# Last cross attention: the output product from rounded halves, and one softmax normalisation handed from VectorE to ScalarE

## The reference

```python
q = (x @ Wq).reshape(B, Sq, h, d).transpose(0, 2, 1, 3)
k = (context @ Wk).reshape(B, -1, h, d).transpose(0, 2, 1, 3)
v = (context @ Wv).reshape(B, -1, h, d).transpose(0, 2, 1, 3)
attn = jax.nn.softmax(jnp.einsum('bhid,bhjd->bhij', q, k) * scale, axis=-1)
out = jnp.einsum('bhij,bhjd->bhid', attn, v)
return out.transpose(0, 2, 1, 3).reshape(B, Sq, h * d) @ Wo + bo     # Wo: 512 x 256
```

## Time and profile before

| what | value |
|---|---|
| median of three runs | 1944.19 us (1941.96 to 1944.48) |
| profiled execution: its own time | 1942.46 us |
| its span, first to last instruction | 1940.6 us |
| mean granted TensorE clock | 0.981 |
| PE busy over the span | 1862.6 us (96%) |
| VectorE | 1501.2 us (77%) |
| ScalarE | 1271.0 us (65%) |
| GpSimd | 950.7 us (49%) |

### The profile page before, as it was taken

How to read it: one execution, slowest core, us unless ns; L and a number is a source line. 1 busy time by engine, 2 the same in 40 slices (tenths; PEclk the granted TensorE clock), 3 DMA queues, 4 the chain that set the end, 5 groups by cost and what they waited for, 6 DMA issues and landing times.

```text
span 1940.6 us, 61563 instructions
## 1 busy us (share of the span) xinstructions
PE 1862.6 (96%) x20887; PEld 1636.0 (84%) x20887; DVE 1501.2 (77%) x3438; ACT 1271.0 (65%) x2720; POOL 950.7 (49%) x1616
## 2 busy tenths in 40 slices
PE   6999999999899999889999999969999999999996
PEld 5888888888678888679999999958888888988885
DVE  6777887878478878756666666657999999998986
ACT  2555555555477777557777777747777777777773
POOL 4556655665256667630000000057676767677751
PEclk9999999999899999889999999979999999999998
DMA  8222233222051111265555555421111111111100
GB/s 239 91 89 89 89 106 101 89 89 64 11 178 31 38 38 37 61 242 197 203 194 189 197 203 194 162 82 57 37 37 39 33 42 30 42 32 41 34 16 10
DMA packets 116595, 182.05 MB, mean 94 GB/s; under 512 B 10850, under 2 KB 94562, under 8 KB 116066
## 3 DMA queue, kind: packets, MB, share of 16 engines
q1 hardware_dynamic: 110386, 166.51, 26.8%
q0 software_dynamic: 6144, 14.69, 2.6%
HBM read 127.68 MB, written 53.48 MB: 93 GB/s over the span
## 4 chain that ended last, share of the span: by engine, by line
PE 54%; DVE 2%; DMA 1%; POOL 1%; issue 1%; ACT 0%; SPq 0%; ACTq 0%; DVEq 0%; POOLq 0%
PE ps_quad L1518 11%; PE ps_out L1538 9%; PE ps_quad L182 6%; PE ps_turned L108 4%; PE ps_quad L102 4%; PE ps_out L114 4%; PE ps_proj L1989 3%; PE ps_turned L182 3%; PE ps_quad L1969 3%; PE ps_proj L182 2%; PE ps_proj L1994 1%; PE ps_proj L1526 1%; DMA c_wv<-in_L_xattn_Wv 0%; PE ps_quad L1984 0%; PE ps_proj L1984 0%
## 5 line engine op out<-in xcount | busy, mean ns | idle before, releaser
L1518 PE MATMUL ps_quad<-e_xT,w 128*128 128x128 f32 x2016 | 235.3, 275 | 1.8 <-DVE e_xT L1476 1.8
L1518 PEld LDWEIGHTS ps_quad<-e_xT,w 128*128 128x128 f32 x2016 | 230.4, 192 | 2.2 <-DVE e_xT L1476 2.2
L369 ACT ACTIVATE a_probsT<-ps_quad 125x1792 f32<-125x1792 f32 x96 | 159.9, 1666 | 98.2 <-PE ps_quad L549 98.2
L1658 POOL TENSOR_TENSOR c_held<-minus_half 1x1 f32<-1x1 f32 x32 | 9.6, 302 | 409.8 <-DMA slots<-e_y 407.3
L1433 ACT ACTIVATE e_act_T<-ps_quad,fc_b 128x128 f32<-128x128 f32 x504 | 136.8, 383 | 91.7 <-PE ps_quad L1518 91.5
L126 DVE TENSOR_SCALAR c_probs<-c_probs,c_recip 112x375 f32<-112x375 f32 x256 | 163.2, 678 | 4.6
L134 ACT ACTIVATE c_probs<-ps_quad,c_negmax 112x375 f32<-112x375 f32 x256 | 143.6, 570 | 32.8 <-DVE c_negmax L119 32.8
L1538 PE MATMUL ps_out<-e_w2H,e_aH 128*128 128x256 f32 x504 | 149.0, 296 | 7.6 <-DVE e_w2L L1464 7.5
L1464 DVE TENSOR_TENSOR e_w2L<-w,e_w2H 128x1024 fp32r<-128x1024 f32 x126 | 150.4, 1235 | 0.0
L119 DVE TENSOR_REDUCE c_negmax<-ps_quad 112x2 f32<-112x750 f32 x128 | 113.9, 930 | 42.4 <-PE ps_quad L102 42.4
L434 DVE TENSOR_REDUCE a_negmax<-ps_turned 112x2 f32<-112x750 f32 x128 | 120.1, 939 | 34.0 <-PE ps_turned L535 33.8
(11 more groups left out here) (356 smaller groups left out, 6008.9 us busy)
## 6 DMA issues: line engine op xcount, KB each, us to landing
w<-in_fc_t SPq DMA_DIRECT2D x71, 1024.0 KB, 4.9
slots<-a_zeros SPq DMA_DIRECT2D x60, 512.0 KB, 4.9
a_cT<-in_ctx_t SPq DMA_DIRECT2D x32, 375.0 KB, 3.5
c_cT<-in_ctx_t SPq DMA_DIRECT2D x32, 375.0 KB, 3.2
e_xg<-slots SPq DMA_DIRECT2D x63, 128.0 KB, 3.9
slots<-e_y SPq DMA_DIRECT2D x63, 128.0 KB, 1.8
out<-c_fo SPq DMA_DIRECT2D x32, 112.0 KB, 1.9
residual<-in_x SPq DMA_DIRECT2D x1, 2912.0 KB, 19.3
```

The lines of the kernel that those rows point to most:

```text
L369: act.activation(probsT[:, 2 * i:2 * i + 2, :, :].rearrange("p c r x -> p r c x"), quad[0:KC, :, 0:2 * HALF].rearrange("p r (c x) -> p r c ...
L1518: last = pe.matmul(hidden[par][:, c // 4, (c % 4) * TILE:(c % 4 + 1) * TILE], mem["w1"][:, par, k, c * 128:(c + 1) * 128], xT[par][:, k, : ...
```

## The change

The copy `oT` becomes two tiles: ScalarE rounds the weighted sum to `oH` at the same place of its turn, and VectorE takes `oL = ps_out - oH` by a subtraction that stands between `xn` and `quantise`. The weights `Wo` are split once, at the start of the stage, into `woH` (ScalarE) and `woL` (VectorE). `out_product` becomes twelve products of halves. Of unit 3, VectorE keeps the reciprocal; the two scalings go to ScalarE, behind the exponential of unit 1.

```diff
+    def dve_reciprocal(self, dve, u):
+        dve.reciprocal(self.recip[:, u, :], self.sums[:, u, :]).then_inc(self.recip_ready, 1)
+
+    def act_normalise(self, act, u):
+        for j in range(2):
+            p = self.probs[u][:, j, :]
+            last = act.activation(p, p, ACT.Copy, scale=self.recip[:, u, j:j + 1])
+        last.then_inc(self.scaled, 1)
...
-        oT = sb("oT", [128, 4, T])
+        oH, oL = (sb(n, [128, 4, T], F32R) for n in ("oH", "oL"))
+        woH, woL = (sb(n, [128, 4, D], F32R) for n in ("woH", "woL"))
...
@@ ScalarE
                     if isinstance(b, int) and b == -2:
+                        act.wait_ge(weights_in, 16 * len(loads))
+                        act.activation(woH[:, :, :], wo[:, :, :], ACT.Copy).then_inc(wo_high, 1)
...
                         core.act_exp(act, 1)
+                    if exists(b - 1):
+                        act.wait_ge(core.recip_ready, 4 * b)
+                        core.act_normalise(act, 3)
...
-                        act.activation(oT[:, :, :].rearrange("p k t -> p (k t)"), psum["out"][:, 0:4 * T], ACT.Copy).then_inc(o_ready, 1)
+                        act.activation(oH[:, :, :].rearrange("p k t -> p (k t)"), psum["out"][:, 0:4 * T], ACT.Copy).then_inc(o_high, 1)
@@ VectorE
+                    if isinstance(b, int) and b == -1:
+                        dve.wait_ge(wo_high, 1)
+                        dve.tensor_tensor(woL[:, :, :], wo[:, :, :], woH[:, :, :], ALU.subtract).then_inc(wo_split, 1)
...
-                        core.dve_normalise(dve, 3, 4 * b + 4)
+                        core.dve_reciprocal(dve, 3)
...
                         norm.dve_apply(dve, b + 3, xn[:, :], row(residual, b + 3))
+                    if exists(b):
+                        dve.wait_ge(o_high, b + 1)
+                        wait(dve, op_mm, b)
+                        dve.tensor_tensor(oL[:, :, :].rearrange("p k t -> p (k t)"), psum["out"][:, 0:4 * T],
+                                          oH[:, :, :].rearrange("p k t -> p (k t)"), ALU.subtract).then_inc(o_ready, 1)
                     if exists(b - 1):
                         quantise(b - 1, 0)
@@ TensorE
-                    for k in range(4):
-                        last = pe.matmul(to[0:T, 0:D], oT[:, k, :], wo[:, k, :], start=(k == 0), stop=(k == 3))
-                    last.then_inc(op_mm, 1)
+                    chain(pe, to[0:T, 0:D], [pair for k in range(4) for pair in split_terms((oH[:, k, :], oL[:, k, :]), (woH[:, k, :], woL[:, k, :]))])\
+                        .then_inc(op_mm, 1)
...
-                        pe.wait_ge(core.probs_ready, 4 * b)
+                        pe.wait_ge(core.scaled, b)
```

More of the change, by code:

```diff
@@ L95, in __init__ @@
         self.recip_ready, self.probs_ready, self.turned_ready = sem("recip_ready"), sem("probs_ready"), sem("turned_ready")
+        self.scaled = sem("scaled")
         self.spread_act, self.values_ready = sem("spread_act"), sem("values_ready")
@@ L1582, in cross_last @@
         mx = {n: sb(f"mx_{n}", [T, D // MX if n in ("scale", "inv") else D]) for n in ("scale", "inv", "t", "magic", "q", "d")}
+        woH, woL = (sb(n, [128, 4, D], F32R) for n in ("woH", "woL"))
+        wo_high, wo_split, o_high = sem("wo_high"), sem("wo_split"), sem("o_high")
         weights_in, c_in = sem("weights_in"), [sem("c_in0"), sem("c_in1")]
@@ L2042, in step @@
                         pe.wait_ge(o_ready, b - 1)
+                        if isinstance(b, int) and b == 2:
+                            pe.wait_ge(wo_split, 1)
                         if exists(b + 1):
@@ L2065, in step @@
                     if exists(b - 1):
-                        pe.wait_ge(core.probs_ready, 4 * b - 1)
+                        pe.wait_ge(core.probs_ready, 3 * b)
                         if exists(b - 1):
@@ L2192, in step @@
                     if exists(b):
-                        pe.wait_ge(core.probs_ready, 4 * b + 2)
+                        pe.wait_ge(core.probs_ready, 3 * b + 2)
                         if exists(b + 1):
@@ L2219, in step @@
                     if exists(b):
-                        pe.wait_ge(core.probs_ready, 4 * b + 1)
+                        pe.wait_ge(core.probs_ready, 3 * b + 1)
                         if exists(b):
```

## The result

The changed kernel takes 2062.5 us (median of 4 runs, 2061.73 to 2064.83) against 1944.1 (4 runs of the kernel before, 1941.96 to 1944.48): a ratio of 1.0614, 95% interval 1.0601 to 1.0627. It is 6% slower, as forecast in direction and inside the range of 2012 to 2082 (and in the likeliest case's own, 2020 to 2070), but 16.5 us over the 2046 forecast. The profiled execution took 2063.01 us, its span 2061.2, with a mean granted clock of 0.960.

A forecast was written before the change was run, and what follows sets the result against it. TensorE, without a gap at 19.56 us a pass, bounds the kernel; the change closes a longer cross-engine chain. 1942.46 + 91.6 (chain) + 4 (last passes) + 7.5 (clock) = 2046 us, range 2012 to 2082.

The forecast's parts named there:

- the likeliest case: Middle passes: VectorE's wait for oH lengthens each pass and the clock sometimes falls; 2046 us, bounds 2020 to 2070, chance 0.70.
- The chain: Unit 3's scores to its next scores, through oH, subtraction, rounding, maxima and ScalarE's scalings: 22.72 us a pass, adding 91.6 us.
- The second rival: On VectorE, unit 2's normalisation runs free of GpSimd, 0.74 instead of 1.84 us; 2006 us in all, chance 0.09.
- The third: Rival: TensorE stays the bound in the middle passes and only the shorter output product counts; 1930 us, chance 0.05.
- a fall in every second pass: TensorE's clock drops to half after its 2.4 us pause in half of 29 passes, 0.52 us each; 7.5 us.
- The cover: TensorE's slack before unit 3's turn, after 6.27 us of work from xd: hides 1.12 of a fall's 1.64 us.
- The sign of about 1 us ahead of the turn of unit 3: In the profile after, TensorE would idle about 1 us before turning unit 3, released by ScalarE.
- the first rival: TensorE's clock falls in every pass, lengthening each of 29 by 0.52 to 1.64 us; 2053 to 2086 us, chance 0.15.
- My argument against it: Against clock falls in every pass: TensorE's pause is one of 2.4 us in 22.7 and it is dense otherwise.
- The start: Splitting the weights into woH and woL falls into idle stretches of 4.17 and 4.62 us; costed at nothing.
- The tail: Passes behind the middle 29: the wait comes twice more and TensorE's 3.09 us pause grows; 4 us, bounds 0 and 6.3.
- The output product: On TensorE, twelve products of halves take some 1.6 us instead of 1.98; its own pass becomes about 19.2 us.

The follow-up runs named there:

- the kernel with both waits moved: Changed kernel with the subtraction behind the rounding, VectorE's unit 3 reciprocal and ScalarE's scaling moved early; 1936.3 us, ratio 0.9955 against the kernel before.
- the last two kernels: Changed kernel with the subtraction behind the rounding: one with unit 3's reciprocal and scaling moved early, 1936.3 us; one with VectorE scaling unit 3, 1936.7 us.

## Why the prediction came out as it did

**The chain was right, term by term.** In the pass without a fall, from scores at 1715.46 to scores at 1738.24, the nine terms can be read off the rows above (forecast in brackets): to the copy of key tile 2, 7.73 (7.77); copy and `oH`, 0.92 (0.92); handover and subtraction, 0.57 (0.70); rounding, 4.80 (4.78), undisturbed, as its second step took 0.21 us; `xd` to the maximum, 2.83 (2.84); maximum to ScalarE's scalings, 3.25 (3.32); the scalings, 0.99 from start to next instruction (0.82); copy of unit 2 and handover, 0.88 (0.83); turn, 0.81 (0.74). The sum is 22.78 against 22.72. That it is so close is partly luck: ScalarE's scalings took 0.17 us more than forecast, the handover with the subtraction 0.13 less. The experiments that move the subtraction show that it is this chain that counts. The second rival (normalisation free of GpSimd) fell: 1.83 us. The third fell: VectorE waited 3.27 us for `oH`.

**The mis-sized term is the clock.** The step that failed is "I take a fall in every second pass: 29 x 0.5 x 0.52 = 7.5 us". The clock fell in 24 of 28 passes. The cover was mis-sized too: TensorE's work from `xd` to the turn of unit 3 was 7.40 - 0.50 = 6.90 us, not 6.27, so only 0.50 us of a fall is covered and not 1.12. The sign of about 1 us ahead of the turn of unit 3 shows as these 0.50 us, and only in the passes without a fall. A fall lengthened that way by 8.39 - 6.90 = 1.49 us in the pass shown, by 1.10 to 1.51 over the 24 (1.64 forecast), and the pass by 23.50 - 22.80 = 0.70 on average (0.52 forecast). All passes together lost 678.04 - 29 x 22.80 = 16.8 us to it, 9.3 more than forecast; filling the pause gave 17.8 back. The truth lies near the first rival, the clock falling in every pass. The Trainium skill describes in "TensorE: Matmul & The Clock Gate", section "HAM oscillation — how this bites in real kernels", a matmul loop that waits for a transfer in every turn, by its figure some 3 to 5 us, and starts each turn at the low clock. The trace agrees with this pattern in 24 of 28 passes, at shorter pauses of 2.28 to 2.45 us. My argument against it, that TensorE is dense otherwise, did not hold.

**The rest of the miss.** The chain's 0.08 us are 2.3 us over 29 passes; with the 9.3 that is the 11.7 us by which the passes were under-forecast. The start, costed at nothing, was 5.8 us later at pass 2. Of this 3.6 us were there before the stage begins, at an instruction that the change does not touch, in the kernel before at 1278.57 us and in the changed one here:

```profile
1282.15 1.09 PE L1977 MATMUL ps_out<-ident,e_wf 128*128 128x128 f32 x4 [7.32 <-DVE e_wf L1327]
```

In the kernel with both waits moved the same instruction comes earlier:

```profile
1278.32 1.08 PE L1977 MATMUL ps_out<-ident,e_wf 128*128 128x128 f32 x4 [7.32 <-DVE e_wf L1327]
```

It varies by that much among executions that share all the code ahead of it, so these 3.6 us are not the change's. The other 2.2 us come in passes 0 to 2. The two halves of the weight were hidden: VectorE still stood idle 2.87 us behind `woL`. Most of the 2.2 goes with the exchange: from the instruction above to the scores of unit 3 in pass 2 are 56.41 us in the kernel before, 58.60 in the changed one, but 56.61 in the changed kernel without the exchange (1279.96 to 1336.57; one execution of each). In the changed one unit 3's turn waits for ScalarE twice there:

```profile
1320.97 0.88 PE L109 MATMUL ps_turned<-ident,c_probs 112*125 112x112 f32 x6 [0.71 <-ACT c_probsT L140]
...
1339.94 0.88 PE L109 MATMUL ps_turned<-ident,c_probs 112*125 112x112 f32 x6 [0.57 <-ACT c_probsT L140]
```

**The tail was right in its sum, partly by luck.** It grew by 4.0 us, as forecast. The pause that was to grow by one wait with its subtraction, 3.09 us in the earlier trace rows, grew by 3.4, to 6.46, and the one ahead of it, 0.34 before, by 1.3, which the forecast had only in its bound. TensorE's work there gave 0.7 back, 0.6 of it in its two output products (1.65 and 2.86 us instead of 1.89 and 3.24):

```profile
2029.23 0.41 PE L2009 MATMUL ps_quad<-ident,c_xd 112*128 112x112 f32 x2 [1.68 <-DVE c_xd L1327]
...
2043.26 0.63 PE L2009 MATMUL ps_quad<-ident,c_xd 112*128 112x112 f32 x2 [6.46 <-DVE c_xd L1327]
```

**The output product** took 1.38 + 0.28 = 1.66 us at full clock, where 1.6 was forecast, and TensorE's own pass is 19.22 (19.2), as the last two kernels show.

## What to carry to other kernels

When an instruction that waits for another engine is put into an in-order queue, the price is neither its length nor the sum of busy times, but the chain that it closes from one pass to the next: add up that chain in rows, and put the instruction behind whatever the next pass hangs on. A pause that such a chain leaves on TensorE is to be priced twice, once as idle time and once as the clock that falls behind it, and on this case's 24 of 28 passes the second price should be taken in every pass unless a row says otherwise. Where two branches join, taking work off one is worth only its lead over the other; here leaving out the same exchange was worth 3.7 us or 22.

## What the runs showed of the hardware that was not expected

- A pause of 2.28 to 2.45 us that comes back every 23.4 us was followed by half clock in 24 of 28 passes; with 1.96 us of it filled, in none of 28 (granted clock 1.00 from 1354.66 to 1992.30 in the kernel with the pause filled).
- The length of the pause does not decide it: 2.39 us was followed by a fall, 2.41 by none. The passes without a fall come 7, 7 and 8 passes apart, and in the passes in between the low stretch moves over TensorE's work from one to the next: from the first to the tenth output product it is 1.16 us at full clock, and 1.28, 1.70, 1.87 and then 2.06 us in the passes from 1752.81 on. What sets this beat stays open.
- VectorE's subtraction of a 448-wide tile began 0.03 us behind ScalarE's end, where 0.1 had been allowed for a handover, and held the queue 0.54 us.
